# The last four experts of tile 3 in two halves of 256 columns, a fourth adapter job, and a tail of two batches

## What is computed

```python
g = einsum('bsd,edf->ebsf', x, Wg)          # eight experts, D = 128, F = 512
u = einsum('bsd,edf->ebsf', x, Wu)
o = einsum('ebsf,efd->ebsd', silu(g) * u, Wd)
shared = (silu(x @ Sg) * (x @ Su)) @ Sd
x2 = x + (1 - sg) * einsum('be,ebsd->bsd', gates, o) + sg * shared
h = relu(x2 @ W1[lang] + b1[lang])          # 128 -> 32
y = x2 + h @ W2[lang] + b2[lang]            # 32 -> 128
out = x2 + (y - mean(y)) * rsqrt(var(y) + eps) * gamma[lang] + beta[lang]
```

## Time and profile before

| what | us |
|---|---|
| median of three runs | 308.05 (307.93 to 308.72) |
| the profiled execution, whole | 308.04 |
| its span, first to last instruction | 306.3 |
| TensorE busy in the span | 301.1 |
| VectorE busy | 260.2 |
| ScalarE busy | 223.0 |
| GpSimd busy | 14.5 |

### The profile page before, as it was taken

How to read it: one execution, slowest core, us unless ns; L and a number is a source line. 1 busy time by engine, 2 the same in 40 slices (tenths; PEclk the granted TensorE clock), 3 DMA queues, 4 the chain that set the end, 5 groups by cost and what they waited for, 6 DMA issues and landing times.

```text
span 306.3 us, 4590 instructions
## 1 busy us (share of the span) xinstructions
PE 301.1 (98%) x1398; PEld 139.0 (45%) x1398; DVE 260.2 (85%) x559; ACT 223.0 (73%) x479; POOL 14.5 (5%) x20
## 2 busy tenths in 40 slices
PE   8999999999999999999999999999999999999995
PEld 2444444444444444444544445444445444444443
DVE  6798999998989898987689997699986799987754
ACT  5797878787888887877667775777777677777640
POOL 0200111100000000000010000101001010000001
PEclk9999999999999999999999999999999999999997
DMA  7990243000000000000000000000000000100001
GB/s 242 421 399 16 49 120 114 0 0 2 1 1 0 2 0 0 0 2 2 0 9 12 0 36 1 0 14 7 34 0 2 10 9 0 37 0 0 3 0 34
DMA packets 8988, 12.10 MB, mean 40 GB/s; under 512 B 3827, under 2 KB 6660, under 8 KB 8964
## 3 DMA queue, kind: packets, MB, share of 16 engines
q1 hardware_dynamic: 8818, 11.68, 11.3%
q10 hardware_dynamic: 146, 0.13, 0.1%
HBM read 10.76 MB, written 1.05 MB: 39 GB/s over the span
## 4 chain that ended last, share of the span: by engine, by line
PE 97%; DVE 2%; issue 0%; DVEq 0%
PE gate_ps L240 10%; PE moe_ps L278 10%; PE moe_ps L276 10%; PE moe_ps L275 10%; PE gate_ps L243 10%; PE gate_ps L246 10%; PE up_ps L261 10%; PE up_ps L264 10%; PE up_ps L258 10%; PE moe_ps L304 1%; PE adapt_ps L298 1%; PE adapt_ps L287 1%; DVE hidden L447 1%; PE x_ps L292 1%; PE x_ps L346 1%
## 5 line engine op out<-in xcount | busy, mean ns | idle before, releaser
L375 ACT ACTIVATE silu<-gate_ps 128x512 f32<-128x512 f32 x144 | 85.8, 596 | 68.0 <-PE gate_ps L246 67.6
L447 DVE SCALAR_TENSOR_TENSOR hidden<-silu,up_ps 128x512 f32<-128x512 f32 x144 | 98.4, 683 | 35.1 <-PE up_ps L264 31.7
L453 DVE TENSOR_TENSOR h_lo<-hidden,h_hi 128x512 f16<-128x512 f32 x144 | 99.1, 688 | 0.1
L380 ACT ACTIVATE h_hi<-hidden 128x512 f16<-128x512 f32 x144 | 89.5, 621 | 2.2 <-DVE hidden L447 2.1
L360 ACT ACTIVATE gx_hi<-x_full,coef 128x128 f16<-128x128 f32 x144 | 55.7, 390 | 0.5 <-DVE coef L534 0.5
L240 PE MATMUL gate_ps<-x_hi,w_hi 128*128 128x512 f16 x144 | 55.1, 383 | 0.0
L243 PE MATMUL gate_ps<-x_lo,w_hi 128*128 128x512 f16 x144 | 55.1, 383 | 0.0
L246 PE MATMUL gate_ps<-x_hi,w_lo 128*128 128x512 f16 x144 | 55.1, 383 | 0.0
L261 PE MATMUL up_ps<-gx_lo,w_hi 128*128 128x512 f16 x144 | 54.8, 381 | 0.1
L258 PE MATMUL up_ps<-gx_hi,w_hi 128*128 128x512 f16 x144 | 54.9, 381 | 0.0
L264 PE MATMUL up_ps<-gx_hi,w_lo 128*128 128x512 f16 x144 | 54.8, 381 | 0.0
(11 more groups left out here) (76 smaller groups left out, 147.9 us busy)
## 6 DMA issues: line engine op xcount, KB each, us to landing
w_full<-weights SPq DMA_DIRECT2D x8, 768.0 KB, 11.2
affine_sb<-affine SPq DMA_DIRECT2D x16, 128.0 KB, 2.9
x_full<-xT SPq DMA_DIRECT2D x4, 256.0 KB, 5.9
w_full<-weights SPq DMA_DIRECT2D x3, 256.0 KB, 4.0
out_dram<-result SPq DMA_DIRECT2D x3, 256.0 KB, 2.0
w2b_sb<-w2b SPq DMA_DIRECT2D x16, 16.5 KB
w_sb<-w SPq DMA_DIRECT2D x16, 16.0 KB
b_sb<-b SPq DMA_DIRECT2D x16, 0.1 KB
```

The lines of the kernel that those rows point to most:

```text
L375: nc.scalar.activation(cols(silu, n % 2, N), gate_ps[n % 2][:, :], ACT.Silu, scale=1.0 / W_SCALE).then_inc(silu_ready, 1)
L380: nc.scalar.activation(cols(h_hi, n % CHUNKS, N), cols(hidden, n % 2, N), ACT.Copy).then_inc(h_hi_ready, 1)
L447: nc.vector.scalar_tensor_tensor(out=cols(hidden, n % 2, N), in0=cols(silu, n % 2, N), scalar=HIDDEN_RESCALE, in1=up_ps[n % 2][:, :], op0= ...
L453: nc.vector.tensor_tensor(cols(h_lo, n % CHUNKS, N), cols(hidden, n % 2, N), cols(h_hi, n % CHUNKS, N), ALU.subtract).then_inc(h_lo_ready, 1)
```

## The change

Steps 0 to 127 stay whole. The last four experts of tile 3 are done twice, at half width: 16 steps for its columns 0 to 255 (batches 0 and 1), then 16 for columns 256 to 511 (batches 2 and 3), which makes 32 steps of 256 columns, 128 to 159. The second half adds up in the other bank, `moe_ps[0]`, and the sum of its first experts comes to it through x2T. gx parts for these steps are made in every second step, in four slots instead of three.

The first half's adapter becomes a fourth job (`JOBS`, two batches, starting at step 147), with `adapter_back` three steps behind its start and the results two steps apart; its store is issued by SP before the tail. The tail keeps batches 2 and 3. Its beta is added on DVE from a transpose in PSUM, not through TensorE.

In all jobs and in the tail `w1` is laid out with 64 columns a batch, zero beyond 32, and adapter weights, biases and h are stacked by twos: even batches on partitions 0 to 63, odd ones from 64 on. One relu serves two batches (in the tail one each), and the row of ones comes out of relu, from zero weights and a bias preset to 1 on GpSimd, for which SP waits before it loads adapters. `adapter_back` writes even and odd batches to two banks and also waits for the copy of x2. Mean and variance come from bn_aggr, one per batch, with one addition of epsilon, in place of six small instructions.

Four products of zeros (512 columns, into an idle bank) are added on TensorE: one ahead of the last product of the last `down`, two behind it, and one ahead of the tail's back products.

The diff, cut to its core (the same renaming runs through gate, up, silu, hidden and their slices):

```diff
 GROUPS = [(t, e) for e in range(NE) for t in (0, 1)] + [(2, e) for e in range(NE)] + [(3, e) for e in range(NE)]
-STEPS = [(t, e, f) for t, e in GROUPS for f in range(CHUNKS)]
+WHOLE = [(t, e, f, 0, N) for t, e in GROUPS[:len(GROUPS) - SPLIT] for f in range(CHUNKS)]
+HALVES = [(TILES - 1, e, f, at, HALF) for at in (0, HALF) for e in range(NE - SPLIT, NE) for f in range(CHUNKS)]
+STEPS = WHOLE + HALVES
 LAST = len(STEPS) - 1
...
-JOB_AT = [DOWN_STEP[0] + 1, DOWN_STEP[0] + 21, DOWN_STEP[2] + 1]
+def group_of(n):
+    return GROUPS.index(STEPS[n][:2])
+def down_step(t, at):
+    return max(n for n, s in enumerate(STEPS) if s[0] == t and s[3] <= at < s[3] + s[4]) + LAG
+JOBS = [(0, 0, BATCHES, down_step(0, 0) + 1), (1, 0, BATCHES, down_step(0, 0) + 21),
+        (2, 0, BATCHES, down_step(2, 0) + 1), (TILES - 1, 0, BATCHES // 2, down_step(TILES - 1, 0) + 1)]
+TAIL = (TILES - 1, BATCHES // 2, BATCHES // 2)
+def back_at(j):
+    return 4 if JOBS[j][2] == BATCHES else 3
+BEFORE = [sum(job[2] for job in JOBS[:j]) for j in range(len(JOBS) + 1)]
 GX_AT = {}
-for g in range(2, len(GROUPS)):
+for g in range(2, len(GROUPS) - SPLIT):
     for q in range(BATCHES):
         GX_AT.setdefault(max(CHUNKS * (g - 1) - 1 + q, 0), []).append((g, q))
+for k in range(2 * SPLIT):
+    for i in range(BATCHES // 2):
+        GX_AT.setdefault(len(WHOLE) + CHUNKS * (k - 1) + 2 * i, []).append(
+            (len(GROUPS) - SPLIT + k % SPLIT, k // SPLIT * BATCHES // 2 + i))
 GX_AT[1] = [(1, 0), (1, 1)]
...
+        back_ps = [adapt_ps, x2_ps]
         coef_ps = x2_ps
         last_tile = TILES - 1
-        last_moe_ps = moe_ps[last_tile % 2]
-        tail_in_ps = [adapt_ps, moe_ps[0], x2_ps, last_moe_ps]
-        tail_y_ps = gate_ps + up_ps
+        last_moe_ps = moe_ps[0]
+        tail_in_ps = [adapt_ps, moe_ps[1]]
+        tail_x2_ps = [x2_ps, gate_ps[1]]
+        tail_y_ps = [gate_ps[0], up_ps[0]]
+        idle_ps = up_ps[1]
...
+            for j, (t, first, count, _) in enumerate(JOBS):
+                if t < last_tile:
+                    sp.wait_ge(back_done, j + 1)
+                    load_adapter(t + 1)
+                sp.wait_ge(result_ready, BEFORE[j + 1])
+                sp.dma_start(out[t, :, first:first + count].rearrange("s b h -> s (b h)"),
+                             result[:, t * N + first * S:t * N + (first + count) * S]).then_inc(stored, 16)
+            sp.wait_ge(result_ready, B - 1)
+            sp.dma_start(out[last_tile, :, BATCHES - 2], cols(result, B - 2, S)).then_inc(stored, 16)
+            sp.wait_ge(stored, 16 * (len(JOBS) + 2))
...
+                t, e, f, at, width = STEPS[n]
+                hi, lo, psum = expert_w(w_hi, e, 2, f), expert_w(w_lo, e, 2, f), moe_bank(t, at)[:, at:at + width]
+                hi_slot, lo_slot = h_slot(h_hi, n), h_slot(h_lo, n)
                 if f == 0 and t == 0:
                     pe.wait_ge(w_lo_ready, 3 * e + 3)
                 if f == 0 and e == 0 and t > 1:
                     pe.wait_ge(x2T_ready, t - 1)
-                start, stop = e == 0 and f == 0, e == NE - 1 and f == CHUNKS - 1
+                if f == 0 and at > 0:
+                    pe.wait_ge(x2T_ready, 3)
+                start = f == 0 and e == (NE - SPLIT if at > 0 else 0)
+                stop = e == NE - 1 and f == CHUNKS - 1
                 pe.wait_ge(h_hi_ready, n + 1)
-                nc.tensor.matmul(psum, hi, cols(h_hi, f, N), start=start, stop=False)
-                nc.tensor.matmul(psum, lo, cols(h_hi, f, N), start=False, stop=False)
+                nc.tensor.matmul(psum, hi, hi_slot, start=start, stop=False)
+                nc.tensor.matmul(psum, lo, hi_slot, start=False, stop=False)
+                if n == LAST:
+                    pe.wait_ge(hidden_ready, n + 1)
+                    nc.tensor.matmul(idle_ps[:, :], warm[:, 0:P], warm[:, :], start=True, stop=True)
                 pe.wait_ge(h_lo_ready, n + 1)
-                nc.tensor.matmul(psum, hi, cols(h_lo, f, N), start=False, stop=stop).then_inc(down_done, 1)
...
+            def adapter_in(j):
+                t, first, count, _ = JOBS[j]
+                pe.wait_ge(x2T_ready, j + 1)
                 pe.wait_ge(adapter_loaded, 16 * 3 * BATCHES * (t + 1))
-                if t > 0:
-                    pe.wait_ge(y_ready, BATCHES * t)
-                    pe.wait_ge(x2_ready, t)
-                for q in range(BATCHES):
-                    last = nc.tensor.matmul(cols(adapt_ps, q, S, A), cols(w1_sb, q, A), cols(x2T, q, S),
+                if j > 0:
+                    pe.wait_ge(y_ready, BEFORE[j])
+                    pe.wait_ge(x2_ready, j)
+                for q in range(first, first + count):
+                    last = nc.tensor.matmul(stacked(adapt_ps, q, S), cols(w1_sb, q, TALL), cols(x2T, q, S),
                                             start=True, stop=True)
                 last.then_inc(adapt_done, 1)
                 pe.wait_ge(consts_ready, 1)
-                for q in range(BATCHES):
+                for q in range(first, first + count):
                     last = nc.tensor.transpose(cols(x2_ps, q, S), cols(x2T, q, S), ident[:, :])
                 last.then_inc(x2_transposed, 1)
...
+            def adapter_back(j):
+                _, first, count, _ = JOBS[j]
+                pe.wait_ge(adapt_h_ready, BEFORE[j + 1] // 2)
+                pe.wait_ge(x2_ready, j + 1)
+                for q in range(first, first + count):
+                    last = nc.tensor.matmul(cols(back_ps[q % 2], q // 2, D), stacked(adapt_h, q, S, A + 1),
+                                            stacked(w2b2_sb, q, D, A + 1), start=True, stop=True)
                 last.then_inc(back_done, 1)
             pe.wait_ge(warm_ready, 1)
...
-            for q in range(BATCHES):
-                pe.wait_ge(x2T_ready, last_tile + q + 1)
-                nc.tensor.matmul(tail_in_ps[q][0:A, 0:S], cols(w1_sb, q, A), cols(x2T, q, S),
+            _, first, count = TAIL
+            tail = list(enumerate(range(first, first + count)))
+            pe.wait_ge(hidden_ready, LAST + 1)
+            for _ in range(2):
+                nc.tensor.matmul(idle_ps[:, :], warm[:, 0:P], warm[:, :], start=True, stop=True)
+            pe.wait_ge(y_ready, BEFORE[-1])
+            for i, q in tail:
+                pe.wait_ge(x2T_ready, len(JOBS) + i + 1)
+                nc.tensor.matmul(stacked(tail_in_ps[i][:, 0:S], q % 2, S), cols(w1_sb, q, TALL), cols(x2T, q, S),
                                  start=True, stop=True).then_inc(adapt_done, 1)
-            for q in range(BATCHES):
-                nc.tensor.matmul(tail_y_ps[q][:, 0:D], cols(x2T, q, S), ident[:, :], start=True, stop=False,
+            for i, q in tail:
+                nc.tensor.transpose(tail_x2_ps[i][:, 0:D], cols(x2T, q, S), ident[:, :]).then_inc(x2_transposed, 1)
+            for i, q in tail:
+                nc.tensor.matmul(tail_y_ps[i][:, 0:D], cols(x2T, q, S), ident[:, :], start=True, stop=False,
                                  is_transpose=True)
-                pe.wait_ge(adapt_h_ready, BATCHES * last_tile + q + 1)
-                nc.tensor.matmul(tail_y_ps[q][:, 0:D], cols(adapt_h, q, S, A + 1), cols(w2b2_sb, q, D, A + 1),
+            nc.tensor.matmul(idle_ps[:, :], warm[:, 0:P], warm[:, :], start=True, stop=True)
+            for i, q in tail:
+                pe.wait_ge(adapt_h_ready, BEFORE[-1] // 2 + i + 1)
+                nc.tensor.matmul(tail_y_ps[i][:, 0:D], stacked(adapt_h, q, S, A + 1), stacked(w2b2_sb, q, D, A + 1),
                                  start=False, stop=True).then_inc(back_done, 1)
-
-            pe.wait_ge(affine_loaded, 16 * B)
-            for q in range(BATCHES):
-                beta = slice((last_tile * BATCHES + q) * 2 * D + D, (last_tile * BATCHES + q + 1) * 2 * D)
-                nc.tensor.matmul(cols(x2_ps, q, S), cols(x2T, q, S), ident[:, :], start=True, stop=False,
-                                 is_transpose=True)
-                last = nc.tensor.matmul(cols(x2_ps, q, S), adapt_h[A:A + 1, q * S:(q + 1) * S],
-                                        affine_sb[A:A + 1, beta], start=False, stop=True)
-            last.then_inc(x2_transposed, 1)
...
+            def adapter_relu(j):
+                t, first, count, _ = JOBS[j]
+                act.wait_ge(adapt_done, j + 1)
                 act.wait_ge(adapter_loaded, 16 * 3 * BATCHES * (t + 1))
-                for q in range(BATCHES):
-                    nc.scalar.activation(cols(adapt_h, q, S, A), cols(adapt_ps, q, S, A), ACT.Relu,
-                                         bias=b1_sb[:, q:q + 1]).then_inc(adapt_h_ready, 1)
-                act.wait_ge(x2_transposed, t + 1)
-                if t > 0:
-                    act.wait_ge(x2_beta_ready, t)
-                    act.wait_ge(y_ready, BATCHES * t)
-                nc.scalar.activation(x2[:, :], x2_ps[:, :], ACT.Copy).then_inc(x2_ready, 1)
+                for pair in range(first // 2, (first + count) // 2):
```

(66 more changed lines are left out.)

226 lines of the change are left out of this document (95 added, 131 removed).

## The result

The changed kernel takes 305.46 us (median; 305.11 to 305.68) beside 308.05 us before: a ratio of 0.9915, with a 95% interval of 0.9903 to 0.9926. It is 0.85% faster. The execution with the profile took 305.68 us, its span is 303.9 us, and 1.8 us lie around it, as before.

What follows compares the result with a forecast made beforehand. TensorE was taken as the bound. Terms of 0.2, 1.8, 1.0 and 0.5 us put the last down product at 299.1; a 7.7 us tail and 1.74 us around the span gave 308.5 us, range 306.8 to 309.7.

Steps and rivals of the forecast that it cites:

- What bounds the kernel: Whole kernel: TensorE ends the chain and is 97% of the 306.3 us span; other engines count only where it waits.
- part 2: Fourth job on TensorE: two batches of tile 3 through adapter and back inside the stretch, +1.8 us; jobs 0 to 2 unchanged.
- if the blocks shrink: Sign against the prediction: adapter and back blocks of jobs 0 to 2 shorter than 1.49 and 1.08 us.
- rival A: Adapter and back passes of odd and even batches overlap: 3.1 us at most, 2.1 likelier, 306.4 us; chance 0.13.
- 1, half products: Last four experts: 288 products of 256 columns at 0.1085 us replace 144 of 512 at 0.2155, +0.2 us.
- term 4: Chain from last up to last down product: shorter links, but less TensorE work hides them; exposed part 0.06 to 0.55, +0.5 us.
- term 3: Steps 151 to 159: job parts among half steps make VectorE late, 8.8 us of work against TensorE's 7.8; +1.0 us.
- The tail, 7.25 for 7.7: Last down product to end of span: two batches left, 7.7 us against 10.68, with results waiting for rstd.
- That one is on the path, 0.22 us: Tail: the fourth zero product, ahead of back, delays back by 0.22 us; the other three cost nothing.
- rival B: Last steps and tail: VectorE not late, and rstd 0.5 us shorter with its columns; 307.0 us, chance 0.15.
- C: Half products: weight load sets their pace, 0.113 us or more each, 309.5 us; chance 0.20.
- D: Last steps: VectorE later still through waits ahead of short instructions and bn_aggr costing as much as statistics; +0.9, 309.4 us, chance 0.10.

Runs made afterwards that it cites:

- whole-step tail: The change without half steps and fourth job, four batches in its tail, statistics before bn_aggr, no zero product ahead of back: 303.62 us, ratio 0.984.

## Why the prediction was wrong

**What bounds the kernel** was right: TensorE holds 94% of the chain after (the page's chain), and each part moved the time by what it moved on TensorE's path.

**The step that failed** is in part 2: "Jobs 0 to 2 keep the number of passes ... I take 0", with bounds of -0.8 to +0.1 us a job. The runs give -0.84 us a job, at the lower end. The forecast plus that alone is 308.5 - 2.5 = 306.0 us, and with the tail's 0.45 us 305.5, which is what was measured (305.46). The runs showed in its place that the passes of an even and an odd batch run at the same time (0.66 and 0.65 us for a block of eight, against 1.06 to 1.09 with all batches in one place). The sign was named too: "if the blocks shrink". The mechanism was there, as rival A, at a chance of 0.13 and 306.4 us. Two judgements were off. The chance rested on "No row shows two at once", but the kernel before could not show it: there all batches lay in the same partitions. A trace is evidence against a mechanism only where the mechanism had a chance to act. And of the 3.1 us at most I took two thirds, "since both passes of one batch share a place"; but the other place holds both passes of the other batch, and the rows show four pairs for eight passes, the full half. By the Trainium skill (TensorEngine Tiling (Array Packing), Key Properties) different tiles load and multiply in parallel; the traces agree, with eight passes in 0.66 us for 1.06.

**The five terms.** Of the +3.56 us ahead of the tail:

| term | predicted | measured |
|---|---|---|
| 1, half products | +0.2 | 287 x 0.1093 - 143 x 0.2155 = +0.55 |
| 2, job 3 on TensorE | +1.8 | 0.19 + 0.64 + 0.09 + 0.42 = +1.34 |
| 3 and 4, VectorE late, last chain | +1.5 | waits 1.76, less 0.11 before: +1.65 |
| sum | +3.5 | +3.54 |

(0.1093 is what remains of the stretch for each half product once the 9 whole ones, job 3 and the waits are taken off.) That the sum came out is partly luck. In the kernel without stacking, where the passes go one after another as forecast, job 3 costs 0.19 + 0.85 + 0.17 + 0.61 = 1.82 us, just the 1.8 forecast; there the stretch is 4.0 us longer, not 3.5. Half products and waits were priced 0.5 us too low, and the pairing that I had put at nothing took 0.48 off job 3 (0.64 and 0.42 for 0.85 and 0.61). The half product was taken from the fp32 passes at 0.1085; 0.8 ns more, 287 times, are 0.2 us, and the count from start to start another 0.1. Terms 3 and 4 were right in mechanism. With the results in the tail, where VectorE isn't late at the end, 0.47 us of exposed chain remain (term 4: 0.55, and 0.5 beyond the kernel before), so about 1.3 of the 1.76 us are lateness (term 3: 1.0). VectorE's `hidden` of step 151 starts at 286.10, that of 159 at 295.27, 9.2 us (forecast 8.8), with next to no idle time until 294.4; `up` waits for gx_lo at 156. The move of the results into the tail confirms the lateness: 0.92 of the 1.76 us went.

**The tail**, 7.25 for 7.7: rstd is shorter with two columns, 0.69 us for 1.01, which gives 0.32 of it; the sum had kept 1.01, and rival B had taken 0.5 off it, in proportion to the columns. "That one is on the path, 0.22 us", of the fourth product of zeros, was right (7.0 us without it), also in the whole-step tail. Its reason was incomplete: the second relu starts 0.39 us after the first and not 0.22 (297.85, 298.24), so back for the second batch would come at 1.99 us in any case, and only the first gains.

**The rivals.** B (VectorE not late) fell. C: half products go at 0.1093, nearer to the fp32 row of the tail than to 0.113; it didn't decide. D (VectorE later still, by 0.9 us) came in part: VectorE took 9.2 us for the stretch and not 8.8. The price that D had for bn_aggr did not come: it is 0.17 to 0.18 us long; in the tail it starts 0.34 us after the statistics it waits for (299.20, 299.54), and what follows starts 0.10 later.

## What to carry to other kernels

Small products that use at most half of the array's rows or columns should be laid out so that neighbours lie in different halves: here, with fp32 products of two passes, it was worth 2.5 us of 308 in three jobs, all that the change gained; other kinds of products were not tried. Before work is brought forward from a tail, compare it with a tail that is merely tightened: here the tail's half cost 3.4 us ahead of the end and saved 2.7 behind it, since TensorE is the bound and half steps leave VectorE too little slack for the small parts; with the last of these moved back into the tail it broke even, no more. In a tail, issue independent instructions ahead of dependent ones (four statistics, then four bn_aggr: 0.55 us), and put a product that fills a wait only where the wait is: ahead of the back products it cost 0.22 us.

## What the runs showed of the hardware that was not expected

- Passes of one instruction list that lie in different halves of the array start together even where the list has two of the same half next to each other (154.14 and 154.16 us with the batches in the order 0, 2, 1, 3). The Trainium skill (PSUM — Partial Sum Buffer, Engine vs sequencer instructions) says that products start and complete in program order; the block of 0.66 us and the paired starts differ from it, and the measurement decides for the starts. Ends are modelled in the trace and say nothing.
- rstd (a power on GpSimd) takes 1.01 us for four columns and 0.69 for two: an estimate from these two is 0.37 us fixed and 0.16 a column.
- The granted clock fell to 1.2 GHz at 297.2 us, within the tail, in the profiled execution of one kernel (two beta passes then took 0.79 us, not 0.48), and only at the end in that of another with the same busy time of TensorE. Between executions of one kernel it differs as well: of 17 of the kernel before, two had a mean granted clock of 0.987, not 0.990 to 0.995, and took 1.8 us more than the median. Why is open.
- The same instructions reach job 0 at 147.13 us in some executions and at up to 147.71 in others.
